# The first half group of the Mamba scan: decay spread and scans before the convolution, gate projections before the third raw projection

## The chip, the core and the metric

The kernel runs on one core of one Trainium2 chip. The metric is the device time of one execution in microseconds (us); lower is better. TensorE (PE), VectorE (DVE), ScalarE (ACT) and GpSimd (POOL) each work off an instruction list of their own, in order, and wait for each other on semaphores. SyncE (SP) only issues DMAs.

## What is computed

Four layers over 2048 tokens of width 256 (2 x 1024), each a layer norm followed by an attention-like branch and a feed-forward branch that are both added to x. The change touches only the attention-like branch of the third layer, a Mamba block. Cut to what matters:

```python
zxbcdt = (hidden_states @ W_in + b_in) * mup_vector
z   = zxbcdt[..., :2048]               # the gate
xBC = zxbcdt[..., 2048:4608]           # x, B and C, "raw" below
dt  = zxbcdt[..., 4608:]
xBC = silu(causal_conv(xBC, conv_w, taps=4) + conv_b)
x, Bm, Cm = split(xBC)                 # 32 heads x 64, 8 groups x 32, 8 groups x 32
dt = softplus(dt + dt_bias)
a  = exp(dt * -exp(A_log))
states = associative_scan(a, dt * x * Bm)      # along the sequence
y = einsum(states, Cm) + D_param * x
y = y * silu(z)
y = group_norm(y) * norm_w
out = y @ W_out + b_out
```

## The kernel before, in words

The program is a list of stages. A barrier of all engines stands ahead of the stage `MambaScan`, which takes some 630 us of the span: it begins at 1808.6 us, when the ternary feed-forward part of the third layer (lines 2230 to 2348) has ended. What the scan needs of dt and a (the tables `Ra` and `Rp`, running products of the decays) has been made beside that feed-forward part and is ready at the barrier.

`MambaScan` works in 32 steps n (`N`), called half groups: batch b = n // 16, head group g = n // 2 % 8, half c4 = n % 2 of the 1024 tokens. Each n has pieces of work on each engine, called kinds. In the order of the data:

- `raw` (b, i, tt): a projection of 128 channels i for 512 tokens tt on PE (line 1780, two matmuls, four records in the trace), evicted by ACT with scale and bias into `RAW` (line 1916). `RAW` has two buffers, and the one of a channel tile is free again when the third tap of the tile two places before is done. Tiles come in the order 16, 0, 18, 1, 2, 3, ...: 16 holds B, 18 holds C, 0 and 1 are x of the first head group. The "third raw projection" is tile 18.
- `raw` on POOL (line 2085): the first tap of the convolution, over 1024 tokens. `tap` 1 to 3 on DVE (line 1990): the other taps. `silu` on ACT (line 1923).
- `sel` on POOL (lines 2093 and 2095): two casts that make the selection matrices `selA` and `selP` of a head group.
- `scan` on PE (line 1794): two matmuls of `selA` with `Ra`, which spread the decays of the heads over the partitions. `scan` on DVE (line 1997): the running product over them, into `LT`. There are two of each for a half group. The diff's scans are these.
- `bt` (lines 1787 and 1929): B transposed. `xd` (lines 1803 and 2004): x transposed and multiplied with dt. `cb` (lines 1819, 1936, 2032, 2101): C times B. `cp` on PE (line 1808) and DVE (lines 2016 and 2018): C with decays. `bd` (DVE, line 2025).
- `st` (line 1842), `h` (lines 2041 and 2045), `within` (line 1862), `across` (line 1880), `end` (line 2054): states and outputs of the half group.
- `gate`: a projection on PE (line 1826) like `raw`, silu and eviction by ACT (line 1943) into `Z`, and a product on POOL (line 2107).

PSUM: `raw`, `gate`, `var` and `out` take turns in a ring of two banks (`A`); `bt`, `cb`, `scan`, `xd` and `cp` in a ring of three (`B`). A bank is free when the engine that empties it is done (`take`, line 1752).

The order on each engine is written out by hand as due times in `AT` (line 1638): a kind of half group n is due at n plus its place, and `order` (line 1690) sorts the kinds of each engine by that number. It is an order only; nothing waits for a time. At the head of the stage the lists are:

```
PE    raw 16, raw 0, raw 18, raw 1, scan 0a, bt, bt, scan 0b, xd, cb, xd, raw 2, cp, scan 1a, raw 3, st, gate 0a, ...
DVE   taps of 16, of 0, of 18 and 1 in turn, scan 0a, scan 0b, xd, xd, bd, cb, cp, scan 1a, taps of 2, h ...
ACT   raw 16, raw 0, raw 18, raw 1, silu 16, 0, 18, 1, bt, bt, cb, raw 2, raw 3, gate 0a, gate 0b, ...
POOL  raw 16, raw 0, sel 0, raw 18, raw 1, cb, raw 2, sel 2, raw 3, ...
```

(`scan 0a` and `0b` are the two scans of n = 0; `raw` on PE and ACT is two steps of 512 tokens.)

Of the kernel before, what the change touches and what calls it, by code (L numbers as in the profile page):

```python
# [454 lines left out]
class Heads0(Stage):  # L455
# [43 lines left out]
    FIRST, PROJ, TURN, OUT, BEGIN = (-0.05, 0.8), (-0.35, 0.5), 0.25, (0.05, 1.05), 0.2  # L499
# [1129 lines left out]
class MambaScan(Stage):  # L1629
# [19 lines left out]
    }  # L1649


    NORM = {"pe": {"turn": (32.5, 32.6, 33.3, 34.2)}, "act": {"xnt": (32.6, 32.7, 33.4, 34.3)},
            "dve": {"stats": (17.0, 18.0, 32.6, 33.6), "rows": (32.0, 32.1, 33.2, 34.0)},
            "pool": {"root": (17.5, 18.5, 32.7, 33.7)}}

    def __init__(self, net, mem, norm, clear):
# [10 lines left out]
        self.raw = {r: i for i, r in enumerate(self.raws)}  # L1667
        beside = [k for kinds in self.NORM.values() for k in kinds]
        self.pn, self.an, self.dn, self.gn = [{s: i + 1 for i, s in enumerate(s for s in o if s[0] not in beside)}
# [20 lines left out]
    def order(self, engine):  # L1690

        at, steps = self.AT[engine], []

        def add(t, *step):
            steps.append((t, len(steps), step))

        for (n, early), b, i, s in self.conv:
            t = n + early
            if "raw" in at:
                for tt in range(1 if engine == "pool" else 2):  # L1700
                    add(t + at["raw"][s], "raw", b, i, *([] if engine == "pool" else [tt]))
            for k in (1, 2, 3):
                if "tap%d" % k in at:
                    add(t + at["tap%d" % k][s], "tap", b, i, k)
            if "silu" in at:
                add(t + at["silu"][s], "silu", b, i)
            if i > 17 and engine in ("pe", "act"):
                for r in range(2):
                    add(t - 1 + .02 * r + (.01 if engine == "act" else 0), "bt", n // 8, r)
        for n in range(self.N):  # L1710
            for kind, places in at.items():
                if kind in ("raw", "tap1", "tap2", "tap3", "silu") or (kind == "sel" and n % 2):
                    continue
                for r, x in enumerate(places):
                    if not (kind == "h" and self.last_chunk(n, r)):
                        add(n + x, kind, n, *([r] if len(places) > 1 else []))
        for kind, places in self.NORM[engine].items():
            for r, t in enumerate(places):
                add(t, kind, r)
        return [s for _, _, s in sorted(steps)]  # L1720
# [1473 lines left out]
```

## Time and profile before

| | us |
|---|---|
| median of 3 runs | 2782.88 (2780.2 to 2784.49) |
| the profiled execution | 2753.76 |
| its span, first to last instruction | 2752.0 |
| PE busy | 2601.9 (95%) |
| DVE busy | 1599.5 (58%) |
| ACT busy | 1064.0 (39%) |
| POOL busy | 926.3 (34%) |

The profiled execution is 29 us below the median of the timed runs. A share of busy time is a mean over stages that have different limits, so the reading below goes by stretches. Times in rows are us from the start of the span.

### The profile page before, as it was taken

Reading aid. Unit: us, or ns where it says so; the run is one execution under the profiler, and the core shown is the slowest. Engines: PE = TensorE matmul, PEld = TensorE weight load, DVE = VectorE, ACT = ScalarE, POOL = GpSimd, SP = SyncE. Lnnn points to the kernel's source line nnn. Section 1 sums busy time; section 2 is a strip of 40 time slices with the busy share of each in tenths; the row PEclk is TensorE's granted clock in tenths of the full one; section 3 lists DMA queues with packets and bytes.
Section 4 is the critical chain, followed back from the end, with each engine's and each line's share of the span. In section 5 each row is a group of like instructions: output and inputs, shape, how many; then the busy total and the mean of one; then the engine's idle time right before and its main releaser. Section 6 shows DMA issues by size and latency. Waiting matters only on the chain.

```text
span 2752.0 us, 41999 instructions
## 1 busy us (share of the span) xinstructions
PE 2601.9 (95%) x16786; PEld 1644.6 (60%) x16786; DVE 1599.5 (58%) x3476; ACT 1064.0 (39%) x1954; POOL 926.3 (34%) x934
## 2 busy tenths in 40 slices
PE   7988988999999999999999998879999999979996
PEld 4445544664556565565665556646666666656896
DVE  6676672226575664756655232767778877754332
ACT  2534553114444534445445111533444444333222
POOL 3221210003232322322222001626666666654222
PEclk8999999999999999999999999989999999989998
DMA  6222211008000000000000200000000000036223
GB/s 191 63 62 63 62 47 62 0 4 148 1 1 1 1 1 1 1 1 1 1 16 1 106 0 31 1 13 17 17 15 16 15 15 17 14 130 190 62 72 134
DMA packets 57139, 109.54 MB, mean 40 GB/s; under 512 B 13793, under 2 KB 32481, under 8 KB 55793
## 3 DMA queue, kind: packets, MB, share of 16 engines
q1 hardware_dynamic: 53152, 96.47, 12.5%
q0 software_dynamic: 3792, 10.39, 1.0%
q8 instruction: 133, 2.18, 0.4%
q14 instruction: 62, 0.50, 0.1%
HBM read 71.16 MB, written 27.08 MB: 36 GB/s over the span
## 4 chain that ended last, share of the span: by engine, by line
PE 86%; DVE 8%; ACT 2%; issue 1%; DMA 1%; POOL 1%; SPq 1%; POOLq 0%; DVEq 0%; ACTq 0%
PE ps L1256 9%; PE ps L1238 8%; PE ps L1780 5%; PE ps L1247 5%; PE ps L1228 5%; PE ps L378 4%; PE ps L1265 4%; PE ps L360 4%; PE ps L365 4%; PE ps L1897 4%; PE ps L1826 4%; PE ps L2914 3%; PE ps L2938 3%; PE ps L697 2%; PE ps L721 2%; PE ps L737 2%
## 5 line engine op out<-in xcount | busy, mean ns | idle before, releaser
L1256 PE MATMUL ps<-back 128*128 128x512 f32 x576 | 292.0, 596 | 0.3 <-ACT back L1299 0.3
L1299 ACT ACTIVATE back<-ps 128x512 f32<-128x512 f32 x288 | 170.0, 597 | 266.3 <-PE ps L1247 264.7
L1294 ACT ACTIVATE back<-ps,front 128x128 f32<-128x128 f32 (+7 forms) x256 | 189.1, 739 | 71.6 <-DVE front L1345 69.5
L1388 POOL TENSOR_TENSOR back<-back 128x512 f32<-128x512 f32 x72 | 91.5, 1271 | 361.7 <-DVE back L1333 361.5
L1247 PEld LDWEIGHTS ps<-front,back 128*128 128x128 f32 x1152 | 140.8, 141 | 118.4 <-issue 95.0
L1398 POOL TENSOR_SCALAR back<-back,front 128x128 f32<-128x128 f32 (+5 forms) x192 | 143.1, 749 | 191.0 <-DVE front L1364 188.3
L809 ACT ACTIVATE back<-ps 128x1024 f32<-128x1024 f32 (+1 forms) x192 | 150.8, 811 | 127.9 <-PE ps L721 127.4
L1345 DVE TENSOR_REDUCE front<-ps 128x1 f32<-128x128 f32 (+7 forms) x256 | 194.0, 758 | 8.8
L1247 PE MATMUL ps<-front,back 128*128 128x128 f32 x1152 | 170.5, 273 | 3.3 <-DVE back L1370 3.3
L1338 DVE TENSOR_TENSOR ps<-ps,front 128x128 f32<-128x128 f32 x256 | 76.0, 297 | 166.1 <-PE ps L1238 166.1
L697 PE MATMUL ps<-rounded 128*128 128x512 f32 (+3 forms) x384 | 140.9, 410 | 12.6 <-DMA rounded<-kh 4.3
L1228 PE MATMUL ps<-front 128*128 128x512 f32 x320 | 152.1, 598 | 0.0
L1238 PE MATMUL ps<-front,back 128*128 128x512 f32 (+3 forms) x384 | 145.5, 490 | 3.4 <-POOL back L1388 3.4
L1780 PE MATMUL ps<-front 128*128 128x512 f32 x320 | 146.7, 602 | 1.9 <-ACT back L1916 1.0
L857 DVE CUSTOM_DVE_ANT_0 ps<-ps,back 128x128 f32<-128x128 f32 (+3 forms) x256 | 120.8, 512 | 44.9 <-PE ps L697 43.7
L931 POOL TENSOR_SCALAR_AFFINE_SELECT back<-back 128x256 f32<-128x256 f32 x128 | 51.8, 408 | 278.4 <-ACT back L809 278.0
L1238 PE MATMUL ps<-back 128*128 128x512 f32 (+3 forms) x384 | 145.0, 486 | 0.0
L320 POOL TENSOR_TENSOR back<-back,front 128x4 f32<-128x4 f32 x8 | 8.1, 1016 | 385.6 <-DVE back L302 385.6
L389 ACT ACTIVATE back<-ps 128x512 f32<-128x512 f32 x64 | 38.2, 597 | 256.1 <-PE ps L360 256.0
L402 DVE TENSOR_TENSOR back<-back,ps 128x512 f32<-128x512 f32 x64 | 44.0, 687 | 151.7 <-PE ps L365 143.4
L1826 PE MATMUL ps<-front 128*128 128x512 f32 x256 | 127.0, 618 | 0.0
L1256 PEld LDWEIGHTS ps<-back 128*128 128x128 f32 x576 | 96.1, 190 | 48.5 <-issue 29.2
(320 smaller groups left out, 5562.8 us busy)
## 6 DMA issues: line engine op xcount, KB each, us to landing
whole<-l_w SPq DMA_DIRECT2D x32, 512.0 KB, 5.2
front<-back SPq DMA_DIRECT2D x128, 64.0 KB, 2.0
rounded<-qh SPq DMA_DIRECT2D x28, 256.0 KB
rounded<-kh SPq DMA_DIRECT2D x56, 128.0 KB
front<-xg SPq DMA_DIRECT2D x47, 129.0 KB
xg<-front SPq DMA_DIRECT2D x2, 3008.0 KB, 34.1
front<-l_win SPq DMA_DIRECT2D x1, 4640.0 KB, 17.7
front<-l_wgu SPq DMA_DIRECT2D x2, 2048.0 KB, 13.3
```

The source lines that it names most:

```text
L697: t = e.matmul(o[:, 0:n], self.QS[:, s, h, qt], self.KS[:, s, h, 512 * r:512 * r + n], start=True, stop=True)
L809: e.activation(self.PT[j % 2][:, 2 * a:2 * a + 2, c:512], PS[:, 2 * a:2 * a + 2, c:512], ACT.Exp).then_inc(A.sem, 1)
L1228: t = e.matmul(o, W, XNT[:, k, tok], start=(k == 0), stop=(k == 1))
L1238: t = e.matmul(s[:, c:c + m], self.Q[:, h, qt * 128:qt * 128 + 128], self.Kt[G % 2][:, c:c + m], start=True, stop=True)
L1247: t = e.transpose(p[:, h * 128:h * 128 + 128], self.P[n % 2][:, h, j * 128:j * 128 + 128], net.ident)
L1256: e.matmul(PS[:, 7, :], self.V[:, j, G % 4 * 128:G % 4 * 128 + 128], self.turned(("turn", n, j)), start=(j == 0), stop=(j == qt)).then_inc ...
L1294: e.activation(self.P[n % 2][:, h, :nk], s[:, :nk], ACT.Exp, bias=st[:, 0, h:h + 1], scale=1.0, accum_out=st[:, 1, h:h + 1]).then_inc(A.se ...
L1299: e.activation(self.turned(step), self.bank(step), ACT.Copy).then_inc(A.sem, 1)
L1345: e.tensor_reduce(self.st[n % 2][:, 0, h:h + 1], s[:, :nk], AX.X, ALU.max, negate=True).then_inc(D.sem, 1)
L1398: e.tensor_scalar(self.P[n % 2][:, h, :nk], self.P[n % 2][:, h, :nk], self.st[n % 2][:, 3, h:h + 1], 1.0, ALU.mult, ALU.mult).then_inc(S.s ...
L1780: t = e.matmul(p, m.Win[:, k, col:col + 128], XNT[:, k, tok], start=(k == 0), stop=(k == 1))
L1826: t = e.matmul(p, m.Win[:, k, col:col + 128], XNT[:, k, tok], start=(k == 0), stop=(k == 1))
```

## The change

A table `FIRST` is added, and in `order` each due time of n = 0, and of no other n, is moved by its entry. The stage then begins with these lists:

```
PE    scan 0a, raw 16, raw 0, scan 0b, gate 0a, gate 0b, raw 18, raw 1, bt, bt, xd, cb, xd, raw 2, cp, scan 1a, raw 3, st, ...
DVE   scan 0a, scan 0b, taps of 16, of 0, of 18 and 1 in turn, xd, xd, bd, cb, cp, scan 1a, taps of 2, h ...
ACT   raw 16, raw 0, gate 0a, gate 0b, raw 18, raw 1, silu 16, 0, 18, 1, bt, bt, cb, raw 2, raw 3, ...
POOL  sel 0, raw 16, raw 0, raw 18, raw 1, cb, raw 2, sel 2, raw 3, ...
```

From `within` of n = 0 on, every list is the one of before. No instruction is added or dropped in the source, and no wait is rewritten: each piece brings its own waits to its new place. No DMA is moved, since SP has its own list, without due times.

```diff
@@ -1649,6 +1649,8 @@
     }
 
 
+    FIRST = {"pe": {"scan": -1.45, "gate": -2.4}, "act": {"gate": -2.4}, "dve": {"scan": -1.45}, "pool": {"sel": -0.7}}
+
     NORM = {"pe": {"turn": (32.5, 32.6, 33.3, 34.2)}, "act": {"xnt": (32.6, 32.7, 33.4, 34.3)},
             "dve": {"stats": (17.0, 18.0, 32.6, 33.6), "rows": (32.0, 32.1, 33.2, 34.0)},
             "pool": {"root": (17.5, 18.5, 32.7, 33.7)}}
@@ -1713,7 +1715,8 @@
                     continue
                 for r, x in enumerate(places):
                     if not (kind == "h" and self.last_chunk(n, r)):
-                        add(n + x, kind, n, *([r] if len(places) > 1 else []))
+                        early = 0 if n else self.FIRST[engine].get(kind, 0)
+                        add(n + early + x, kind, n, *([r] if len(places) > 1 else []))
         for kind, places in self.NORM[engine].items():
             for r, t in enumerate(places):
                 add(t, kind, r)
```

## Rows read from the trace of the kernel before

**Rows 1.** The page: the chain that ended last, shares of the span by engine.
```profile
PE 86%; DVE 8%; ACT 2%; issue 1%; DMA 1%; POOL 1%; SPq 1%; POOLq 0%; DVEq 0%; ACTq 0%
```

**Rows 2.** Busy time by stretch: length, busy us per engine, granted clock (1.00 is 2.4 GHz), DMA.
```profile
1800.00:1804.00 4.00, 4.00 (x18) 3.29 (x16) 0.00 (x0) 0.00 (x0) 0.00 (x0) 0.58 0.00 0
1836.00:1840.00 4.00, 4.00 (x23) 2.71 (x24) 2.83 (x5) 0.39 (x1) 0.50 (x1) 0.50 0.40 98
1843.20:1861.80 18.60, 17.25 (x294) 9.97 (x293) 18.11 (x25) 6.14 (x8) 6.18 (x6) 1.00 0.07 16
1861.80:1900.00 38.20, 37.60 (x560) 25.37 (x560) 30.84 (x52) 16.87 (x29) 27.23 (x21) 1.00 0.10 23
```

**Rows 3.** Timeline of PE: start, us, what, [idle before and who ended it].
```profile
1798.96 8.75 PE L2265 MATMUL ps<-rounded 128*128 128x256 f32 x48 [3.33 <-issue]
1808.60 10.57 PE L1780 MATMUL ps<-front 128*128 128x512 f32 x24 [0.90 <-DVEq L176]
1820.14 3.70 PE L1780 MATMUL ps<-front 128*128 128x512 f32 x8 [0.98 <-ACT back L1916]
...
1828.21 1.97 PE L1787 MATMUL ps<-front,back 128*128 128x128 f32 x8 [4.13 <-ACT back L1923]
1834.28 0.80 PE L1794 MATMUL ps<-rounded 128*128 128x256 f32 x2 [4.10 <-DVE back L1997]
1834.87 1.05 PE L1803 MATMUL ps<-front 128*128 128x128 f32 x4
...
1837.81 5.14 PE L1780 MATMUL ps<-front 128*128 128x512 f32 x8
1842.39 0.80 PE L1808 MATMUL ps<-rounded 128*128 128x256 f32 x2
...
1851.91 1.98 PE L1826 MATMUL ps<-front 128*128 128x512 f32 x4
...
1861.97 0.69 PE L1862 MATMUL ps<-back 64*64 64x64 f32 x32 [0.60 <-DVE back L2054]
```

**Rows 4.** Timeline of DVE.
```profile
1814.55 4.66 DVE L1990 SCALAR_TENSOR_TENSOR back<-back,front 128x1024 f32<-128x1024 f32 x3 [6.06 <-POOL back L2085]
1819.14 5.01 DVE L1990 SCALAR_TENSOR_TENSOR front<-back,front 128x1024 f32<-128x1024 f32 x3
...
1827.02 1.28 DVE L1990 SCALAR_TENSOR_TENSOR front<-back,front 128x1024 f32<-128x1024 f32 x1 [1.67 <-POOL front L2085]
...
1833.00 1.22 DVE L1997 TENSOR_TENSOR_SCAN back<-ps,back 128x512 f32<-128x512 f32 x1
1835.11 1.22 DVE L1997 TENSOR_TENSOR_SCAN back<-ps,back 128x512 f32<-128x512 f32 x1 [0.89 <-PE ps L1794]
...
1843.22 0.17 DVE L2016 COPY back<-ps 128x8 f32<-128x8 f32 x1 [2.88 <-PE ps L1808]
```

**Rows 5.** Timeline of ACT.
```profile
1691.82 1.28 ACT L2296 ACT_TABLE_LOAD   x1
1712.17 0.60 ACT L2296 ACTIVATE back<-ps 128x512 f32<-128x512 f32 x1 [19.07 <-PE ps L2247]
...
1810.68 0.78 ACT L1916 ACTIVATE back<-ps,front 128x512 f32<-128x512 f32 x1 [13.62 <-PE ps L1780]
...
1833.12 1.15 ACT L1923 ACTIVATE front<-front 128x1024 f32<-128x1024 f32 x1
```

**Rows 6.** Timeline of POOL.
```profile
1813.32 1.13 POOL L2085 TENSOR_SCALAR back<-back,front 128x1024 f32<-128x1024 f32 x1 [4.60 <-ACT back L1916]
...
1818.10 1.59 POOL L2093 CAST rounded<-rounded 128x512 fp32r<-128x512 f32 x1
1819.64 1.39 POOL L2095 CAST rounded<-rounded 128x256 fp32r<-128x256 f32 x1
...
2180.67 0.62 POOL L2093 CAST rounded<-rounded 128x512 fp32r<-128x512 f32 x1
2181.22 0.41 POOL L2095 CAST rounded<-rounded 128x256 fp32r<-128x256 f32 x1
```

## The prediction

> **What bounds the kernel now.** I read the shares of the chain that ended last, then the stretches at the head of the scan stage, then each engine's timeline there. Over the whole span the chain is on PE for 86% and on DVE for 8% [rows 1], which says nothing yet about the one place that the change touches. The stretches do [rows 2]. From 1861.80 on PE is busy for 37.60 of 38.20 us: the rest of the stage is bound by PE. From 1843.20 to 1861.80 DVE is busy for 18.11 of 18.60 us and PE for 17.25: there DVE is the bound, and at its end PE has stood idle for 0.60 us until DVE delivers the outputs of the first half group (1861.97 in [rows 3]). Ahead of 1843.2 neither is full. The first data have to go through PE, ACT, POOL and six taps on DVE [rows 4], PE stands for 4.13 and 4.10 us [rows 3], and at 1843.22 DVE has waited for 2.88 us for `cp` from PE [rows 4]. So the reader has to follow the change in three pieces: the chain to `cp` at 1842.4, the DVE stretch to 1861.8, and the rest.
>
> A time t below is counted from 1808.60, when the barrier lets PE go.
>
> **1. PE waits for `sel`.** Its first instruction is now `scan 0a`, which needs the selection matrices of POOL. Those two casts are recorded in two lengths: 1.59 and 1.39 us, or 0.62 and 0.41 [rows 6]. The long pair lies beside a run of taps on DVE, and the short pair isn't beside one; at the barrier DVE has nothing to do. I take the short pair: 0.1 us of a small memset ahead of it (estimated), 0.55 from cast to cast, 0.41, so PE starts at about t = 1.2. `scan 0a` itself is 0.8 us at the low clock [rows 3], taken as 0.25 of PE's time at the high one, and the first raw step begins at 1.45 where it began at 0. The other end is the long pair: 2 us more. Queued behind this wait is everything on PE.
>
> **2. DVE's taps wait for `scan 0b`.** DVE's list now has both scans ahead of the taps, and PE gives the second only behind four raw steps. Six steps took 10.57 us and two took 3.70 [rows 3], so one is 6.87 / 4 = 1.72 us. Four end at t = 1.45 + 6.9 = 8.3, `scan 0b` reaches DVE at about 8.85, and it takes 1.22 there [rows 4]: DVE is free at 10.1. The taps of tile 16 would have been ready long before: they started at 5.95 (1814.55, [rows 4]), and with the delay of part 1 at 7.4. So they start 4.15 us later than before.
>
> **3. The taps themselves get a little shorter.** Before, six of them took from 1814.55 to 1824.15, 9.6 us, where six times 1.28 is 7.7 [rows 4]: some were stretched while POOL worked beside them. `sel` is no longer there; the first tap of tile 18 on POOL still is. I give back about 1.0 us, so that the six take 8.6 and end at 18.7, 3.1 us later than the 15.55 of before. Ends: 7.7 and 9.6, that is +2.2 and +4.1.
>
> **4. The gates fill a gap of PE.** `gate 0a` and `0b` are 1.72 us each behind other steps of the kind, at t = 8.55 to 12.0. ACT evicts about 2.08 us after a step begins (1808.60 and 1810.68, [rows 3, 5]) in 0.78 us, so bank and engine are free for tile 18 at 12.0, its first step is ready at 14.1, and its buffer is free at 14.1 too, when tap 3 of tile 16 ends. Tile 1 is ready at 19.2, while ACT gets to its second step at 19.4. The gates are therefore just hidden; one microsecond more ahead of them would show. Silu needs a table, and its load of 1.28 us comes ahead of `gate 0a` now. In [rows 5] such a load starts at 1691.82, at once behind the work before it, and its activation runs at 1712.17, when PE delivers: a load doesn't wait with its activation. Here it lies at 9.45 to 10.75, and the gate is ready at 10.65, so it costs 0.1 us. The Trainium skill (page "ScalarE: Activation LUTs", section "What ACT_TABLE_LOAD costs") gives a switch of tables 1283 ns and a drain of 1380 ns on top; by that the gate would be evicted at 12.1, tile 1 would be ready some 0.3 us late, and the sum would be 2.8 instead of 2.5 us. No drain stands in the rows.
>
> **5. To the end of the taps.** From the end of the six (1824.15) to tap 1 of tile 1 (1827.02) lie 2.87 us of ACT and POOL, and to 1833.00 five more taps [rows 4]. Nothing there changes: they end at t = 27.5 instead of 24.4, again +3.1.
>
> **6. What the scans give back behind the taps is small.** On DVE they took from 1833.00 to 1836.3 [rows 4]. But `xd` on PE also needs the last silu on ACT, which ended at 1834.27 [rows 5], and PE began `xd` at 1834.87, behind `scan 0b` [rows 3]. So `xd` can come 0.55 us sooner relative to the taps, and not 3.3: the wait for silu takes the place of the wait for the scan. At `xd` the kernel is 3.1 - 0.55 = 2.5 us late.
>
> **7. From `xd` to `cp`** PE runs the same steps, 7.52 us before (1834.87 to 1842.39). The clock there was 0.50 between 1836 and 1840 [rows 2], so 1.2 GHz, after the 4.1 us gaps, and two raw steps took 5.14 us instead of 3.4 to 3.7 [rows 3]. In the changed kernel PE also stands for some 5 us ahead of `xd`, so I take the same clock. The bounds are all of it at 2.4 GHz, about 2.4 us less, and all at 1.2 GHz, about 2.4 us more.
>
> **8. What the gates give back.** They leave PE in the stretch from 1843.2 to 1861.8, 1.98 us each [rows 3], 3.8 together. But DVE is the bound there, with 18.6 - 18.1 = 0.5 us of idle time [rows 2]. Its list is unchanged, and PE only waits longer at 1861.97. I book 0, at most 0.5. Behind that, the lists are those of before and PE is full, so what is late at 1861.8 stays late to the end of the kernel.
>
> **The sum.** Against the profiled execution: +1.45 (head of PE) +2.7 (taps behind `scan 0b`) -1.0 (no `sel` beside taps) -0.55 (scans behind the taps) = +2.6, and -0.1 for the small gains of part 8: +2.5 us, 2753.8 to 2756.3. The three timed runs lie 29 us above the profiled one, and I carry the difference over as it stands: 2782.9 + 2.5, so 2785.4 us.
>
> **The rivals.**
>
> *Slower (I): PE's clock falls at the head.* Before, PE stood for 0.90 us at the barrier; now from 1807.7 to about 1809.8, 2.1 us. Ahead of the barrier is a gap of 3.33 us [rows 3], and the clock was 0.58 from 1800 to 1804 behind it [rows 2]; the gap of 0.98 at 1820.14 was followed by none. 2.1 lies between. If the clock falls, the raw steps run at half speed until it is back: it was low for 3.4 us in the first stretch (0.42 of full speed missing in 4 us, at half speed) and for 5.1 us at least in the second (1834.87 to 1840), so 1.7 to about 3 us are lost, and they go in full through `scan 0b` into the taps. That makes +4.2 to +5.5 with the short casts. With the long ones PE stands for 4.1 us, like at 1828.21, where the clock was low next; then it is 2.5 + 2 + 1.7 to 3 = +6.2 to +7.5, or 2790. This decides over 0.2% from the point where 3.1 us come on top of my sum. The Trainium skill (page "TensorE: Matmul & The Clock Gate", section "Part 1: The HAM clock gate") has the rule behind it: the array's clock is the low one by default, and sustained work raises it. The trace agrees, by the 0.58 and 0.50. Against it: DVE is idle when `sel` runs, and the gap is then shorter than any that was followed by a low clock.
>
> *Faster (II): PE's time counts.* If the DVE stretch has slack that the busy share hides, for example because operations there are themselves waiting in a short chain with PE, the 3.8 us of the gates come back: 2.5 - 3.8 = -1.3 us, 2781.6, and with the full clock of part 7 -3.7 us. Against it: 0.5 us of idle time in 18.6. Even so it stays within 0.2%.
>
> *The taps don't wait (III).* If `scan 0b` reached DVE before the first taps are ready, only parts 1 and 3 would remain: +1.45 - 1.0 - 0.55 = -0.1. That would need PE to deliver it before t = 7.4, and its list puts four raw steps of 1.72 ahead; I give this 5%.
>
> **How the numbers follow.** A change of 0.2%, 5.6 us, is about what a measurement of this kernel can tell from none. Forecast, +2.5 with its bounds of clock and taps (-0.8 to +5.4): 65%. Rival I: 20%, a bit over half of it above 5.6 us. Rival II: 10%. Rival III: 5%. So faster by over 0.2% has 3%, within 0.2% has 84%, slower by over 0.2% has 13%. The range is from 2781, rival II with a little of the clock's gain, to 2790.5, rival I with the long casts.
>
> **What the changed profile would show.** Right: the first record of line 1794 on PE near 1809.8, the two casts at about 1 us together, DVE's second scan at t = 8.9 with the taps at its heels, a table load between `raw 0` and the first gate, DVE's row of line 2016 (`cp`) about 2.5 us after 1843.2, DVE still full in the 18.6 us behind it, and an idle time of PE at line 1862 of 0.6 plus up to 3.8 us. Wrong: casts of 1.6 and 1.4 us at the head, a clock of 0.5 in the first raw steps, or gaps of DVE behind `cp`, which would show that the gates had been on the path. What would break the forecast most easily is the clock at `xd` and `cp`, whose phase can differ by 2.4 us either way from one execution to the next.

## The result and the profile after

| | before | after |
|---|---|---|
| median (8 runs each) | 2781.38 us | 2791.87 us |
| lowest to highest | 2779.48 to 2784.49 | 2786.0 to 2796.06 |
| ratio, 95% interval | | 1.0035, 1.0025 to 1.0046 |
| the profiled execution | 2753.76 us | 2796.06 us |

The kernel became 0.35% slower, 10.5 us, where 2.5 us had been forecast, and it lies above the range (2790.5). The two profiled executions are 42 us apart and can't be compared as wholes: 28.6 of these lie in a stop in the router (the part of the last layer that sends each token to its experts), far behind the scan, which the first profile of before doesn't have (told below). 8.3 lie ahead of the barrier, where the two programs are the same, 4.2 in the scan stage, and 1.2 between it and the router. So the scan stage is read by itself. Times t are again counted from the barrier: in the trace after, that is 1816.9 (the memset in the first row).

POOL's timeline of the kernel after, at the head of the stage:

```profile
1816.91 0.10 POOL L2071 MEMSET back<- 128x6 f32 x1 [9.75 <-DVEq L176]
1816.95 0.61 POOL L2096 CAST rounded<-rounded 128x512 fp32r<-128x512 f32 x1
1817.51 0.40 POOL L2098 CAST rounded<-rounded 128x256 fp32r<-128x256 f32 x1
```

The casts have the short form of [rows 6], one microsecond for both. PE's timeline:

```profile
1818.06 0.56 PE L1797 MATMUL ps<-rounded 128*128 128x256 f32 x2 [2.06 <-POOL rounded L2098]
1818.42 8.67 PE L1783 MATMUL ps<-front 128*128 128x512 f32 x16
1826.53 0.81 PE L1797 MATMUL ps<-rounded 128*128 128x256 f32 x2
...
1847.74 1.09 PE L1806 MATMUL ps<-front 128*128 128x128 f32 x4 [6.53 <-ACT front L1926]
...
1866.40 1.11 PE L1806 MATMUL ps<-front 128*128 128x128 f32 x4 [3.28 <-DVE back L2000]
```

PE has stood for 2.06 us, released by the second cast, and begins at t = 1.16. Four raw steps then take 8.67 us and not 6.9. The stretches say why (length, then busy time of PE, its weight loads, DVE, ACT and POOL, the granted clock, DMA share, GB/s):

```profile
1818.40:1821.60 3.20, 3.20 (x6) 1.36 (x5) 1.22 (x1) 0.00 (x0) 0.00 (x0) 0.50 0.01 3
1821.80:1826.40 4.60, 4.60 (x12) 2.07 (x11) 0.00 (x0) 2.33 (x3) 1.13 (x1) 1.00 0.01 4
1855.40:1873.70 18.30, 15.02 (x261) 9.86 (x259) 17.94 (x24) 4.71 (x6) 6.08 (x6) 0.81 0.07 16
```

PE worked without a pause at 1.2 GHz (0.50) in the first of them and at 2.4 GHz (1.00) in the second. The third is DVE's stretch behind `cp`: DVE is busy for 17.94 of 18.30 us, as before (18.11 of 18.60, [rows 2]), and PE is down from 17.25 to 15.02. DVE's timeline:

```profile
1827.37 1.22 DVE L2000 TENSOR_TENSOR_SCAN back<-ps,back 128x512 f32<-128x512 f32 x1 [7.42 <-PE ps L1797]
1828.51 4.39 DVE L1993 SCALAR_TENSOR_TENSOR back<-back,front 128x1024 f32<-128x1024 f32 x3
...
1855.44 0.17 DVE L2019 COPY back<-ps 128x8 f32<-128x8 f32 x1 [2.21 <-PE ps L1811]
```

DVE waits 7.42 us for the second scan's matmuls, and the taps start right behind it. In times t, beside those of before:

| | before | forecast | after |
|---|---|---|---|
| PE begins | 0 | 1.2 | 1.16 |
| second scan on DVE | 26.5 | 8.85 | 10.5 |
| first tap of tile 16 | 5.95 | 10.1 | 11.6 |
| tap 1 of tile 1 | 18.4 | 21.5 | 23.45 |
| `xd` on PE | 26.3 | 28.8 | 30.8 |
| `cp` of n = 0 on DVE | 34.6 | 37.1 | 38.55 |
| `cp` of n = 1 on DVE | 53.15 | 55.65 | 56.8 |
| `within` of n = 2 on PE | 75.3 | 77.8 | 79.4 |
| `within` of n = 31 on PE | 608.6 | 611.1 | 612.8 |

From the third half group on, the distance stays at 4.1 to 4.2 us to the end of the stage. So the stage accounts for 4.2 of the 10.5 us.

### The profile page after: what moved, and what is told of

Same layout as the page of the kernel before. It is cut to its first block, busy times and chain, and to the rows that moved or that the text cites. A ratio compares the mean times of both kernels' runs of the same rounds, so it can differ in the third digit from the quotient of the medians.

```text
span 2794.3 us, 42000 instructions
## 1 busy us (share of the span) xinstructions
PE 2619.7 (94%) x16786; PEld 1656.0 (59%) x16786; DVE 1599.6 (57%) x3476; ACT 1064.4 (38%) x1954; POOL 921.9 (33%) x934
## 3 DMA queue, kind: packets, MB, share of 16 engines
q1 hardware_dynamic: 53152, 96.47, 12.2%
## 4 chain that ended last, share of the span: by engine, by line
PE 85%; DVE 8%; ACT 2%; issue 1%; another core or an unknown queue 1%; DMA 1%; POOL 1%; SPq 1%; POOLq 0%; DVEq 0%; ACTq 0%
PE ps L1256 9%; PE ps L1238 8%; PE ps L1783 5%; PE ps L1247 5%; PE ps L1228 4%; PE ps L378 4%; PE ps L1265 4%; PE ps L360 4%; PE ps L365 4%; PE ps L1900 4%; PE ps L1829 4%; PE ps L2917 3%; PE ps L2941 3%; PE ps L697 2%; PE ps L721 2%; PE ps L737 2%
## 5 line engine op out<-in xcount | busy, mean ns | idle before, releaser
L697 PEld LDWEIGHTS ps<-rounded 128*128 128x128 f32 x384 | 73.4, 201 | 87.5 <-DVE front L857 37.1
```

The source lines that it names most:

```text
L697: t = e.matmul(o[:, 0:n], self.QS[:, s, h, qt], self.KS[:, s, h, 512 * r:512 * r + n], start=True, stop=True)
```

## The experiments

Theory A, after this trace: the stage loses its 4 us at the head, through PE's wait for `sel`, the low clock that this wait brings, and DVE's wait for `scan 0b`; the gates add nothing and return nothing; what is measured above 4 us comes from elsewhere. Theory B: the change costs more than the stage shows, because it makes a later part of the kernel longer. Theory C: it is the gates that cost. (In the expectations A is called HEAD and B is called TAIL.)

**Each half of the change alone.** The first two kernels are before and after again, on a chip whose executions have no stop in the router. The edits of the other two, in `FIRST`:

```diff
-    FIRST = {"pe": {"scan": -1.45, "gate": -2.4}, "act": {"gate": -2.4}, "dve": {"scan": -1.45}, "pool": {"sel": -0.7}}
+    FIRST = {"pe": {"scan": -1.45}, "act": {}, "dve": {"scan": -1.45}, "pool": {"sel": -0.7}}   # e1_scans_only
+    FIRST = {"pe": {"gate": -2.4}, "act": {"gate": -2.4}, "dve": {}, "pool": {}}                # e2_gates_only
```

> The kernel before once more, for its trace and its spread beside the changed one. Both theories are about where 10 us of the median go, when the trace of the changed kernel shows only 4.1 us of them in the scan stage (its third half group begins 12.4 us later than in the first trace of before, and 8.3 of these lie ahead of the stage). Theory HEAD (the whole loss is in the scan stage, and the rest of the difference between the two traces is luck): this trace has a tail like the changed kernel's, with the stop of 26 us of all engines at the third router, and the time is 2780 to 2784. Theory TAIL (the change makes the tail longer too): this trace has no such stop, or a shorter one, by about 6 us.

> The changed kernel once more. HEAD: 0.15% slower than before (+4 us), the earlier 0.35% having some luck in it. TAIL: +8 to +12 us again, of which 4 from the barrier to the third half group and the rest behind the scan stage.

> Only the spread, the scans and sel of the first half group go early; the gates stay. By my sum it is the scans that cost: PE waits 1.2 us for sel, DVE's taps wait for the second scan; I expect the row of line 2019 (cp) on DVE 2.5 to 4 us late against before and the time +2.5 to +4 us. If instead the gates cost (they delay tile 18, and their absence later leaves PE idle so that its clock falls), this kernel is within 1.5 us of before.

> Only the gates of the first half group go early. By my steps tile 18 and tile 1 come 1.2 us later to ACT (their first rows at t = 12.4 and 15.8), the taps end 1.2 us later, and nothing comes back in the DVE stretch: +1 us. The rival, that gate time is paid on the path later, gives -2.5 us. If the fall of PE's clock in the emptied DVE stretch is what costs, +2.5 to +4 us with a granted clock of 0.5 some 50 to 60 us behind the barrier.

| | median, us | ratio to before | `cp` of n = 1 | `within` of n = 2 |
|---|---|---|---|---|
| before | 2756.8 | | 53.15 | 75.3 |
| after | 2760.5 | 1.0016 (1.0007 to 1.0025) | 57.7 | 79.8 |
| scans only | 2762.6 | 1.0028 (1.0019 to 1.0037) | 57.1 | 80.9 |
| gates only | 2758.6 | 1.0010 (1.0000 to 1.0019) | 53.5 | 77.3 |

The kernel before, run as a kernel of its own beside these, was put at 1.0012 (1.0002 to 1.0023) of itself, so a ratio of this size is at the edge of what the comparison can tell. The two expectations that wanted to tell A from B by the stop couldn't do it here: the trace of before has none, and it took 2757 us where 2780 to 2784 was expected of A. The traces are sharper. In that of after the clock was low from the stage before, so that its first tap came at t = 12.2 and not at 11.6. The scans alone bring 3.95 us at `cp` of n = 1; the gates alone bring 0.35: theory C falls. Gates alone do delay tile 1 as expected (its tap 1 at t = 19.6 against 18.4), but two thirds of it have come back by `cp` of n = 1. Both lose a further 1.7 us between `cp` of n = 1 and the third `within`, where the clock fell for 3.4 us with PE nearly full; of that more below. So the kernel with only the scans early is 5.6 us late at the third `within` and 5.8 in the median, where 2.5 to 4 had been expected, and the one with only the gates early 2.0 and 1.8, where 1 had been. On this chip the changed kernel is 3.7 us slower in the median; its stage shows 4.5 in this pair of traces and 4.1 in the first.

**Where DVE's wait and PE's wait come from.** Two placements of the scans, both with the gates in their old place. `e4_both_first` puts both of PE's scan steps ahead of raw 16; `e5_scans_fit` puts both behind raw 16.

```diff
+    FIRST = {"pe": {"scan": (-1.45, -1.74)}, "act": {}, "dve": {"scan": (-1.45, -1.45)}, "pool": {"sel": (-0.7,)}}   # e4
+    FIRST = {"pe": {"scan": (-1.41, -1.705)}, "act": {}, "dve": {"scan": (-1.45, -1.45)}, "pool": {"sel": (-0.7,)}}  # e5
...
+                    first = .02 if engine == "pe" and (b, i) == (0, 16) else 0    # e5: raw 16 a little earlier than raw 0
```

> The kernel before in the company of the next three, for its trace. If the difference between the first comparison (+0.35%) and the second (+0.16%) belongs to the chip, the two agree again on a chip where all engines but GpSimd stand still for some 25 us in the router (then before takes 2780 or so and its trace has that stop), and the stop is some 6 us shorter here than in the changed kernel. If the difference is chance, the stop has the same length in both.

> The changed kernel once more. From the barrier to within of the third half group (line 1865) 79 to 80 us against 75.3; clock of 0.5 in the first raw steps again, if the 2.05 us that PE waits for sel bring it down each time; +4 us in the median, and +10 us if the stop in the router is there and longer.

> The scans early, as in the kernel with only the scans early, but both of PE's scan steps stand ahead of the first raw step, so that DVE's taps don't wait for the second one behind four raw steps. The gates stay. If that wait is what makes the taps late (part 2 of my sum), they start at t = 9.2 us (7.7 if the clock stays up) against 11.6 of the kernel with only the scans early, tap 1 of tile 1 at about 21 instead of 23.4, and cp of n = 1 at about 54.7 instead of 57.1; what is left against before (53.15) is PE's wait for sel and the low clock. If the loss is in the clock alone, tap 1 of tile 1 stays at 23.

> As the one before, but PE's two scan steps stand behind the first tile's raw steps, so PE doesn't wait for sel at all and its clock has no idle time to fall in. By my sum the taps start at t = 6.6 (before: 5.96), tap 1 of tile 1 at 18.1 (before: 18.4), xd on PE at 25.4 (before: 26.3), and cp of n = 1 is 0.9 us earlier than before: -0.9 us. If early scans cost by themselves, whatever PE does at the head, it is slower than before by 2 us or more.

| | median, us | ratio to before | first tap | tap 1 of tile 1 | `xd` on PE | `cp` of n = 1 |
|---|---|---|---|---|---|---|
| before | 2782.8 | | 5.95 | 18.4 | 26.3 | 52.9 |
| after | 2791.0 | 1.0034 (1.0022 to 1.0046) | 11.6 | 23.45 | 30.85 | 56.9 |
| both first | 2791.9 | 1.0021 (1.0011 to 1.0031) | 9.2 | 21.3 | 28.7 | 56.0 |
| scans fit | 2781.4 | 0.9993 (0.9983 to 1.0003) | 6.3 | 18.4 | 25.8 | 52.9 |

DVE's timeline of the one with both scans first, and of the one that fits them in:

```profile
1815.13 2.34 DVE L2000 TENSOR_TENSOR_SCAN back<-ps,back 128x512 f32<-128x512 f32 x2 [1.84 <-PE ps L1797]
1822.55 4.67 DVE L1993 SCALAR_TENSOR_TENSOR back<-back,front 128x1024 f32<-128x1024 f32 x3 [5.08 <-POOL back L2088]
```

```profile
1815.49 2.34 DVE L2001 TENSOR_TENSOR_SCAN back<-ps,back 128x512 f32<-128x512 f32 x2 [4.14 <-PE ps L1798]
1817.74 4.64 DVE L1994 SCALAR_TENSOR_TENSOR back<-back,front 128x1024 f32<-128x1024 f32 x3
```

In both the two scans run one behind the other, 2.34 us. In the first kernel DVE then waits 5.08 us for POOL's first tap, so the taps are no longer held by the scans, but by PE's late and slow start: 9.2 against 5.95. The second has neither wait, and its taps start 0.35 us behind those of before. That separates the 5.65 us by which the first tap came late: 2.4 are DVE's wait for `scan 0b` (11.6 to 9.2), 2.9 are PE's head (9.2 to 6.3), and 0.35 are the scans themselves. With all three as small as they get, the early scans are worth nothing: `cp` of n = 1 is where it was, and not the 0.9 us earlier that had been expected. The 0.5 us that they save at `xd` is lost again by `cp`, 8.6 us behind `xd` instead of 8.1. The kernel with both scans first misses its expectation too: `cp` of n = 1 at 56.0 and not 54.7. It reaches `xd` 2.2 us before the changed kernel, but needs 8.9 us from there to `cp` of n = 0 instead of 7.7, since its clock is low from t = 22.0 to 35.7 (in the changed kernel from 25.3 to 35.5). Its median shows no gain over the changed kernel.

**PE's idle time and its clock.** `e6_filled` is the changed kernel with work put into PE's wait; the result of the two matmuls is overwritten by `scan 0a` and used by nothing.

```diff
                 p = self.take(w, step, self.B)
+                if step == ("scan", 0, 0):
+                    e.matmul(p, m.Win[:, 0, 2048:2176], XNT[:, 0, 0:512], start=True, stop=True)
+                    e.matmul(p[:, 0:256], m.Win[:, 0, 2048:2176], XNT[:, 0, 0:256], start=True, stop=True)
                 w.wait_ge(self.pooled, self.gn["sel", n // 2 * 2])
```

> The changed kernel, with two matmuls more (512 and 256 columns, into the bank that scan 0a then writes over; their result is used by nothing) ahead of PE's wait for sel, so that PE works for 1.3 of the 2.05 us in which it stood. If that idle time is what brings the clock down at the head, the first raw steps run at 2.4 GHz, the taps start at t = 10.1 instead of 11.6, tap 1 of tile 1 comes at 21.9 instead of 23.45, and cp of n = 1 at 55.3 instead of 56.9: 1.6 us less than the changed kernel. If the clock falls there for another reason (the end of the stage before), nothing changes, or +0.2 us.

PE's timeline and the stretch of its first raw steps:

```profile
1811.60 1.12 PE L1796 MATMUL ps<-front 128*128 128x512 f32 x2 [0.90 <-DVEq L176]
...
1812.81 0.58 PE L1800 MATMUL ps<-rounded 128*128 128x256 f32 x2
1813.23 7.03 PE L1783 MATMUL ps<-front 128*128 128x512 f32 x16
```

```profile
1813.20:1820.20 7.00, 7.00 (x19) 3.17 (x18) 1.22 (x1) 2.33 (x3) 1.12 (x1) 1.00 0.01 4
```

The clock is 1.00, four raw steps take 7.03 us instead of 8.67, the taps start at 10.1, and tap 1 of tile 1 comes at 21.9: all as expected of the idle time as the cause. Across all traces the first raw steps had the low clock in each of the eight in which PE waited 2.05 us for `sel` (in seven it fell there, in one it had been low since the stage before). Where PE didn't wait, they had it only in two, both low since the stage before. But the 1.55 us are not kept: `cp` of n = 0 came at 37.85 against 38.55 to 39.4 in the changed kernel, since the clock was low longer behind `xd`, `cp` of n = 1 at 56.1 (expected 55.3), and the third `within` at 79.0 against 79.5. The median was 2761.4, ratio 1.0014 (1.0001 to 1.0026), beside 2759.9 and 1.0006 (0.9995 to 1.0017) of the changed kernel on this chip, where before takes 2756.1: no gain that the times show.

**The gates in a gap.** `e7_fit_gates` has the scans of `e5` and the gates behind tile 1's raw steps:

```diff
+    FIRST = {"pe": {"scan": (-1.41, -1.705), "gate": (-2.05, -2.15)}, "act": {"gate": (-2.05, -2.2)}, "dve": {"scan": (-1.45, -1.45)},
+             "pool": {"sel": (-0.7,)}}
```

> The scans placed as in the kernel that fits them in behind the first tile's raw steps, and the gates behind tile 1's raw steps, where PE stands for 4 us before the transposes of B. Nothing waits longer for them there: tap 1 of tile 1 at 18.4 and cp of n = 1 at 52.9 as in that kernel, up to 1.4 us less if the clock stays up towards cp. Against it: PE has 3.8 us less to do in DVE's stretch, stands there for 3.3 us, and its clock may fall, which costs 1.6 us later. So -1.5 to +1.5 us against before.

Its median is 2756.2, ratio 0.9999 (0.9986 to 1.0013). So it lies within the -1.5 to +1.5 us that were expected. Its one trace is of its slowest execution, in which the clock was low from the stage before through all of raw 16 (first tap at t = 9.2, where 6.3 was expected), so it doesn't show the placement undisturbed. One thing can be read there: PE stands for 3.29 us in DVE's stretch, as after, and soon after its clock is low for 6.8 us. Neither this kernel nor `e5` beats the one before beyond the intervals.

**What the chips add.** On two chips the change cost 3.7 us (2760.5 against 2756.8, 2759.9 against 2756.1), on two 8.2 and 10.5. The latter are those where an execution takes 25 us more, before and after alike. (No chip is known to have been used in two comparisons, so a property of the chip can't be told from one of its session; "chip" below stands for either.)

> The kernel before, one look, for the same question: 107.8 us (chip without the stop) or 133.5 us (with it) from the router's first matmul to the first expert; the barrier at 1809 us, if the barrier's 1812 to 1817 in the changed kernel's traces is more than chance; anywhere from 1807 to 1817 if it is chance, since nothing ahead of the barrier was changed.

> The changed kernel beside the filled one. Open is why the loss is 4 us on one chip and 8 to 10 on another, with the same 3 to 4 us in the scan stage. If it is the pace of the router that goes with the clock at its start: on a chip whose span has the stop in the router, from the router's first matmul to the first expert 136 us whenever the clock is back 3 us behind that matmul, and 133.5 us when it comes back 5 us behind it; on a chip without the stop 107.8 us in both.

> One more look at the kernel before. On a chip with the stop in the router: first expert 133.5 us behind the router's first matmul if the clock comes back about 5 us behind that matmul, 136 us if it comes back at 3 us, whichever kernel it is. Barrier to the third within: 75.3, or 76.7 where the clock falls once more in DVE's stretch.

> One more look at the changed kernel. If the longer stop belongs to the change, 136 us from the router to the first expert again on a chip with the stop, with the clock back at 3 us; if it belongs to the clock's phase alone, some looks have 133.5. Barrier to the third within: 79.5.

> A second look at the kernel before on the same chip. The barrier lies between 1807 and 1817 us whatever the kernel, if its place is chance; router to first expert by the phase of the clock, as in the first look of this call.

> A second look at the changed kernel on the same chip. Barrier to the third within 79.5 us; router to first expert 136 us with the stop if the longer stop belongs to the change, 133.5 in some looks if it belongs to the phase of the clock alone.

The longest wait in the router of the changed kernel, first trace: engine, line, what it waited for, total, times, longest. Then that of the kernel before, in `e9_before`, from such a chip:

```profile
ACT front L2821 <- remote: 26.2, 1, 26.2
```

```profile
ACT front L2818 <- remote: 22.7, 1, 22.7
```

The stretch of the stop in the first trace after, 24 us behind POOL's first indirect DMA, and one as long in the first trace before, which has no stop, 23 us behind that DMA (columns as in [rows 2]):

```profile
2515.60:2537.40 21.80, 1.54 (x6) 1.14 (x6) 1.61 (x3) 0.32 (x2) 13.19 (x15) 0.50 0.37 128
```

```profile
2501.00:2523.00 22.00, 22.00 (x103) 16.23 (x102) 9.36 (x24) 7.89 (x16) 14.52 (x16) 1.00 0.96 302
```

PE is busy for 1.54 us instead of 22, while POOL goes on issuing its indirect DMAs.

All twelve traces of the two kernels, in us. "Back" is the time from the router's first matmul to the return of PE's clock:

| kernel | barrier at | barrier to `within` of n = 2 | last `within` to router | router to first expert | back | stop |
|---|---|---|---|---|---|---|
| before | 1808.6 | 75.3 | 29.6 | 107.8 | 5.1 | no |
| before (e0) | 1809.7 | 75.3 | 29.6 | 107.8 | 5.2 | no |
| before (e6) | 1810.5 | 76.7 | 30.8 | 108.1 | 5.5 | no |
| before (e3) | 1809.1 | 76.7 | 30.8 | 133.7 | 5.4 | yes |
| before (e8) | 1810.4 | 75.8 | 32.4 | 135.4 | 2.9 | yes |
| before (e9) | 1819.3 | 78.9 | 32.4 | 135.5 | 3.0 | yes |
| after | 1816.9 | 79.4 | 30.8 | 136.3 | 2.9 | yes |
| after (e0) | 1816.6 | 79.8 | 29.5 | 107.8 | 5.1 | no |
| after (e3) | 1811.7 | 79.5 | 30.8 | 136.4 | 3.0 | yes |
| after (e6) | 1808.1 | 79.5 | 32.2 | 108.1 | 2.7 | no |
| after (e8) | 1811.9 | 79.6 | 30.9 | 135.5 | 3.1 | yes |
| after (e9) | 1807.2 | 79.5 | 32.2 | 136.0 | 2.7 | yes |

Column by column: the barrier is at 1811.3 on average before and at 1812.1 after, so, as far as twelve traces tell, its late place in the first trace after was chance. The stage takes 76.4 against 79.6 on average: +3.1, or +4.3 against the best case of before, which the changed kernel never reaches. The router with the stop takes 135.4 us in the kernel before too, when its clock comes back early (with the clock back at 5 us, 133.7 and, in `e5`, 133.3). So the longer stop goes with the phase of the clock and needs no change of the order, and theory B falls in the form in which I had it. Why it goes with the phase isn't shown, and all four traces of the changed kernel with the stop have the early return, against two of three of before. In the pair of `e3` the stop was 2.7 us longer after than before, where some 6 had been expected. On average the router with the stop is 1.2 us longer after than before, 136.05 against 134.9, from four traces and three. That gives 3.1 + 1.2 = 4.3, or 5.5 against the best case, for the chips with the stop. The measured 8.2 and 10.5 have intervals that reach down to 6 and 7.

One pair of traces can be laid out whole. In `e3` both profiled executions lie within 0.1 us of their kernel's median, and they are 8.1 us apart: 2.6 ahead of the barrier, where nothing was changed, 2.8 from the barrier to the third `within`, 2.7 from the router's first matmul to the first expert, and nothing elsewhere. The share of low clock over all timed executions doesn't tell the chips apart: on the chip of `e3` the mean granted clock is 0.9715 before and 0.9690 after, on that of `e0` 0.9772 and 0.9750, which is (as 2 x (1 - clock) x span, an estimate) 14 and 12 us more at 1.2 GHz, where the times differ by 8.2 and 3.7. What lies between 4.3 and the measured differences stays open; a single profile for each timed kernel can't tell whether the changed kernel meets the unlucky phases more often or whether something else is added.

## Why the prediction was wrong, point by point

**Where the 8 us lie.** 2.5 us were forecast and 10.5 measured. 1.7 of the difference are in the stage, at whose end the kernel is 4.2 us late (4.1 at the third `within`). In the order of the sum, the 4.1 are +5.65 where the forecast had +4.15 (first tap), -0.63 for -1.0 (taps), -0.47 for -0.55 (`xd`), -0.64 for 0 (from `xd` to `cp`), -0.24 for -0.1 (DVE's stretch), and +0.46 for 0 (from there to the third `within`; PE comes out of the stretch late by its low clock). The other 6.3 are outside the stage, where the prediction has no term at all.

**Parts 1 and 2, the waits: right in kind, 1.5 us short.** PE's start (1.16 against 1.2) and the short casts were right. The sum took 1.72 us for a raw step in a place where PE's clock is low. This is rival I, to which I gave 20%; the clock has fallen there in every trace with this wait in which it was up before, seven of them. The step that failed is the reading of the gaps: of 0.98 us (no fall) and 3.33 us (fall) I took 2.1 as nearer to the harmless one, for no reason that a row gave, and booked the fall at nothing. A gap that nothing in the trace bounds should have had an even chance, and then the forecast lies near +3.7, midway between 2.5 and the 4.2 to 5.5 of the rival. The rule of the Trainium skill that stood beside this rival (page "TensorE: Matmul & The Clock Gate", section "Part 1: The HAM clock gate"), that the low clock is the default and sustained work raises it, agrees with the filled kernel, by its 1.00 against 0.50. That 2.05 us of idle time are enough for the fall is what the runs show.

**Part 3, the taps: right in kind.** Six taps took 8.9 us (11.6 to 20.5) where 8.6 was forecast and 9.5 stood before. **Part 5: right.** From there to tap 1 of tile 1 it is 2.9 us in both kernels. **Part 4, the gates: right, and tight as said.** They don't show in the changed kernel, where the taps are late. Where the taps are on time, in the kernel with only the gates early, tile 1 is 1.15 us late. The table load lay at 1827.93, behind the last eviction of raw 0, ahead of its activation's data:

```profile
1827.13 0.78 ACT L1919 ACTIVATE back<-ps,front 128x512 f32<-128x512 f32 x1 [0.94 <-PE ps L1783]
1827.93 1.28 ACT L1946 ACT_TABLE_LOAD   x1
1829.22 0.78 ACT L1946 ACTIVATE back<-ps,front 128x512 f32<-128x512 f32 x1
```

The load and its start cost 1.29 us together. There is no drain of the 1380 ns that the Trainium skill adds (page "ScalarE: Activation LUTs", section "What ACT_TABLE_LOAD costs"); the measurement decides here.

**Part 6, the silu in place of the scan: right.** From tap 12 to `xd` 2.6 us, before 3.07: 0.47 saved, 0.55 forecast, and not the 3.3 of two scans. **Part 7, up to `cp`:** 7.7 us against 8.35, inside its bounds. **Part 8, DVE is the bound: right.** `cp` of n = 0 to `cp` of n = 1 takes 18.3 us against 18.5, so of the gates' 3.8 us 0.2 came back. PE's idle time came at `xd` of n = 1 (3.28 us, line 1806) and not at line 1862, where I had looked for it. What I had not thought of is its price: behind it the clock is low for 6.8 us (1866.1 to 1872.9), `gate 1a` takes 2.76 us instead of 1.98, and the third `within` is 4.1 us late where `cp` of n = 1 was 3.7 late. Rival II falls, and so does rival III.

**The carry-over to the median: wrong by some 6 us on this chip, and only in part explained.** This is the larger of the two steps that failed. "What is late at 1861.8 stays late to the end of the kernel" puts everything behind the stage at nothing, and I added the stage's sum to the median as it stood. Through the rest of the stage that holds (4.1 to 4.2 us throughout), and on the chips without the stop about for the whole kernel (3.7 in both medians, 4.5 and 2.9 at the third `within` in their pairs of traces). There the number itself would have passed for right, but partly by luck: the head was 1.5 us too cheap in the sum, and from `xd` to `cp` the clock gave back 0.6 that nobody had booked. On the chips with the stop more is added, of which the traces explain about one microsecond by the longer router; the cause of the rest stays open.

## What to carry over

To move a step ahead, read what it waits for in its new place and what stands behind it: here 1 us of casts on POOL held up PE, four steps on PE held up DVE, and both engines had ready work behind the wait. A step with a short wait belongs behind the first piece of work that needs nothing, as `e5` does it, and it pays only if something was waiting for it. Work taken from an engine that isn't the bound makes idle time, and on TensorE idle time may be charged twice, at the low clock behind it.

## What had not been expected of the hardware

- An idle time of 2.05 us ahead of PE's work brought the clock down in seven traces of seven in which it had been up; 0.90 us at the same place did in none.
- The clock also fell where PE never stood for more than 0.6 us: in the kernel with only the scans early it was 0.5 from 1866.2 to 1869.6, and in two traces of before at the same spot, at a cost of 1.4 to 1.7 us. In other executions of the same kernel it stayed up there.
- Once low, the clock can stay low under nearly full work: in three traces (`e9_before`, `e0_after`, `e7_fit_gates`) it was 0.50 for 20.5 us across the barrier. In the first of them that is from 1804.7 on, and PE was busy for 13.10 of 14.00 us in this stretch of it:

```profile
1806.00:1820.00 14.00, 13.10 (x49) 11.04 (x50) 1.57 (x3) 0.00 (x0) 0.10 (x1) 0.50 0.00 1
```

  The same 48 matmuls took 12.65 us there and 8.75 us in [rows 3].
- On some chips, here in three of five comparisons, PE, ACT, DVE and SP nearly stand still in stretches while POOL issues its 32 indirect DMAs in the router (PE busy for 1.54 of 21.80 us in the first trace after), which then takes 25 to 29 us longer than on the others, with single waits of 10 us between engines and up to 26.2 us on ACT. On the others the same DMAs, as many and as fast (about 1 us each on POOL), cost nothing. What makes a chip do this was not found.
